# Counting out-degrees with node numbers split into 64 low and 100 high values, with three table copies on ScalarE

## The chip, the cores and the metric

The kernel runs on one core of one Trainium2 chip. The metric is the device time of one launch in microseconds (us). The time before is the median of three runs.

## The reference, cut to what matters

Four graph layers run one after the other on a graph of 6,250 nodes and 100,000 edges sorted by destination. The change touches only what the first layer needs of the sources: how many edges leave each node (`out_deg`), and the node features scaled with it.

```python
h = jnp.maximum(_layernorm(x, axis=-1), 0.0)
...
out_deg = jax.ops.segment_sum(ones_e, src, num_segments=N)
norm_src = jnp.clip(out_deg, 1.0, None) ** (-0.5)
h = nfeat * norm_src[:, None]
agg = jax.ops.segment_sum(h[src], dst, num_segments=N)
```

## The kernel before, in words

The program is a row of stages with a barrier between them: `survey` (statistics of the graph), `sort_edges` (skipped for sorted input), `tables` (the stage of the change), `gather_first` (the first layer over edge tiles), then three more layers. A stage is written out engine by engine; each engine works through its own list in order, and semaphores hold it where it needs another's result. A wait therefore also holds everything that stands behind it in the same list.

`tables` does three things at once.

**The out-degree counter.** The 100,000 source numbers lie as 125 partitions by 800 columns. A number is split in a low part (7 bits, 128 values) and a high part (50 values). The columns go in 50 groups (`GR`) of 16 (`W`). For each group VectorE makes two tables of zeros and ones in bf16: `low` (125 x 128 x 16, L457) and `high` (125 x 50 x 16, L459). TensorE then multiplies, for each of the 16 columns, `low[:, :, k]` (stationary, 128 columns wide) with `high[:, :, k]` (moving, 50 columns; L429) and adds everything up in one PSUM tile: row = low part, column = high part, value = out-degree. Both tables have two buffers. The semaphore `built` tells TensorE that a group is ready, `counted` tells VectorE that a group's buffer is free again, so VectorE may be two groups ahead and no more.

**The edge tables.** GpSimd gathers source, destination and type of each edge tile into `raw` by 24 indirect DMAs (L383). When the counter has reached group 30 (`LAY`), VectorE makes the local destinations, a validity mask and the keys out of them (L467 to L478) and copies source and type to floating point (L480, L482). In the groups behind that, 31 to 38, TensorE also transposes one of eight blocks of these tables per group (three transposes, L439) into one of two PSUM buffers `pt`. ScalarE takes them out (L411 to L413, or L407 and L408 for one block) and says so with `taken`; from the third block on TensorE waits for `taken` before it transposes into a buffer that was used:

```python
if b >= 2:
    pe.wait_ge(taken, b - 1)
```

SyncE writes keys and local destinations to DRAM and reads the keys back (L360 to L367); they are read in the next stage.

**The normalised features.** ScalarE squares the features (L395); at group 24 (`EVEN`) VectorE finishes the variance (L463), ScalarE takes the root (L398), at group 26 VectorE makes scale and shift (L485, L486; semaphore `scaled`), and ScalarE writes the normalised features `g.h` in 50 instructions (L401). After the last group VectorE reads the degrees (L488), ScalarE takes the root, VectorE inverts it, and both write the scaled features, which SyncE sends to DRAM in ten transfers (L374). Then the next stage starts.

In ScalarE's list of this stage the order is: squares, root, the 50 normalising instructions, the copies out of the transposed blocks, root of the degrees, scaled features.

Of the kernel before, what the change touches and what calls it, by code (L numbers as in the profile page):

```python
# [5 lines left out]
P = 128  # L6
# [3 lines left out]
NW = 50  # L10
NP = NW * P
# [4 lines left out]
TB = 7  # L16
TA = TB * P
EP, EC = 125, E // 125
# [11 lines left out]
BF16 = mybir.dt.bfloat16  # L30
I32 = mybir.dt.int32
ALU = mybir.AluOpType
# [272 lines left out]
def tables(nc, g, sem, a, early, scratch):  # L305
# [3 lines left out]
    W = 16  # L309
    GR = EC // W  # L310
    B8 = TB + 1
    K = NW // 5
    EVEN, LAY = 24, 30
    with Stage(nc, "od") as od:
        si, part = g.sources, od.sb("part", [EP, EC], I32)
        lo, hi = od.sb("lo", [EP, EC], BF16), od.sb("hi", [EP, EC], BF16)
        lows, highs = od.sb("lows", [EP, P, W], BF16), od.sb("highs", [EP, NW, W], BF16)
        low, high = od.sb("low", [EP, 2, P, W], BF16), od.sb("high", [EP, 2, NW, W], BF16)
    g.acc0 = early.sb("acc0", [P, NW * (2 * D + RELS)])
    with Stage(nc, "tb") as st:  # L320
        raw = st.sb("raw", [P, B8, 3, P], I32)
        rawf = st.sb("rawf", [P, B8, 3, P])
        ok = st.sb("ok", [P, B8, P])
        keys = st.sb("keys", [P, TB, P])
        pads = st.sb("pads", [1, P])
        local = st.sb("local", [P, TB, P], BF16)
# [6 lines left out]
        (dv, built, counted, squared, evened, rooted, scaled, normed, asked, answered, scaled2, sent_a, sent_d,  # L333
         laid, turned, taken, keyed, kept, out) = (
            sem("tb_" + k) for k in ("dv", "built", "counted", "squared", "evened", "rooted", "scaled", "normed",
                                     "asked", "answered", "scaled2", "sent_a", "sent_d", "laid", "turned", "taken",
                                     "keyed", "kept", "out"))
        got = [sem(f"tb_got{k}") for k in range(3)]
# [6 lines left out]
        with nc.Block() as block:  # L345
            @block.sync
            def _(sp):
# [8 lines left out]
                sp.wait_ge(out, 64)  # L356
                sp.wait_ge(keyed, 1)
                for b in range(TB):
# [21 lines left out]
            def _(pool):  # L380
                for k in (1, 0, 2):
                    for b in range(B8):
                        pool.indirect_dma_start(raw[:, b, k, :], None, g.edges_d.rearrange("k (e one) -> (k e) one", one=1),  # L383
                                                bass.IndirectOffsetOnAxis(g.starti[:, b:b + 1], 0),
                                                element_offset=k * (E + P)).then_inc(got[k], 16)
                pool.wait_ge(counted, GR)
                nc.gpsimd.memset(g.acc0[:, :], 0.0)

            @block.scalar
            def _(act):  # L390
                act.wait_ge(evened, 1)
                for v in range(NW):
                    if v >= 4:
                        act.wait_ge(squared, v - 3)
                    nc.scalar.activation(junk[:, v % 4, :], g.x[:, v * D:(v + 1) * D], ACT.Square, bias=less[:, v:v + 1],  # L395
                                         accum_out=var[:, v:v + 1]).then_inc(squared, 1)
                act.wait_ge(evened, 2)
                nc.scalar.activation(rstd[:, :], var[:, :], ACT.Sqrt).then_inc(rooted, 1)  # L398
                act.wait_ge(scaled, 1)
                for v in range(NW):  # L400
# [23 lines left out]
            @block.tensor  # L424
            def _(pe):
                for i in range(GR):
                    pe.wait_ge(built, 2 * (i + 1))
                    for k in range(W):
                        mm = nc.tensor.matmul(ps[:, 0:NW], low[:, i % 2, :, k], high[:, i % 2, :, k],  # L429
                                              start=(i == 0 and k == 0), stop=(i == GR - 1 and k == W - 1))  # L430
                    mm.then_inc(counted, 1)
                    if LAY < i <= LAY + B8:
                        b = i - LAY - 1
                        if b == 0:
                            pe.wait_ge(laid, 1)
                        if b >= 2:
                            pe.wait_ge(taken, b - 1)
                        for k in range(3):
                            t = nc.tensor.transpose(pt[b % 2][:, k * P:(k + 1) * P], rawf[:, b, k, :], g.ident[:, :])  # L439
                        t.then_inc(turned, 1)  # L440

            @block.vector
            def _(dve):
                c = Chain(dve, dv)
                nc.vector.memset(pads[:, :], -5.0)
                nc.vector.tensor_scalar(less[:, :], g.total[:, :], -1.0 / D, None, ALU.mult).then_inc(evened, 1)
                nc.vector.tensor_copy(lows[:, :, :], g.iota[0:EP, :].unsqueeze(2).broadcast_to([EP, P, W]))
                c.step(nc.vector.tensor_copy(highs[:, :, :], g.iota[0:EP, 0:NW].unsqueeze(2).broadcast_to([EP, NW, W])))
                c.step(nc.vector.tensor_scalar(part[:, :], si[:, :], 127, None, ALU.bitwise_and))
                c.step(nc.vector.tensor_copy(lo[:, :], part[:, :]))  # L450
                c.step(nc.vector.tensor_scalar(part[:, :], si[:, :], 7, None, ALU.arith_shift_right))
                c.step(nc.vector.tensor_copy(hi[:, :], part[:, :]))
                for i in range(GR):
                    if i >= 2:
                        dve.wait_ge(counted, i - 1)
                    cols = slice(i * W, (i + 1) * W)
                    nc.vector.tensor_tensor(low[:, i % 2, :, :], lo[:, cols].unsqueeze(1).broadcast_to([EP, P, W]),  # L457
                                            lows[:, :, :], ALU.is_equal).then_inc(built, 1)
                    nc.vector.tensor_tensor(high[:, i % 2, :, :], hi[:, cols].unsqueeze(1).broadcast_to([EP, NW, W]),  # L459
                                            highs[:, :, :], ALU.is_equal).then_inc(built, 1)  # L460
# [3 lines left out]
                    if i == LAY:  # L464
                        dve.wait_ge(got[1], 16 * B8)
                        dl, keep = rawf[:, :, 1, :], ok[:, :, :]
# [8 lines left out]
                        c.step(nc.vector.tensor_tensor(keys[:, :, :], keys[:, :, :], ok[:, 0:TB, :], ALU.mult))  # L475
                        c.step(nc.vector.tensor_scalar(dl, dl, -1.0, None, ALU.add))
                        c.step(nc.vector.tensor_scalar(keys[:, :, :], keys[:, :, :], -1.0, None, ALU.add))
                        nc.vector.tensor_copy(local[:, :, :], rawf[:, 0:TB, 1, :]).then_inc(keyed, 1)  # L478
                        dve.wait_ge(got[0], 16 * B8)
                        c.step(nc.vector.tensor_copy(rawf[:, :, 0, :], raw[:, :, 0, :]))  # L480
                        dve.wait_ge(got[2], 16 * B8)
                        nc.vector.tensor_copy(rawf[:, :, 2, :], raw[:, :, 2, :]).then_inc(laid, 1)  # L482
                    if i == EVEN + 2:
# [3 lines left out]
                dve.wait_ge(counted, GR)  # L487
                nc.vector.tensor_scalar(nsrc[:, :], ps[:, 0:NW], 1.0, None, ALU.max).then_inc(asked, 1)  # L488
                dve.wait_ge(answered, 1)
# [2531 lines left out]
```

## Time and profile before

| | |
|---|---|
| median of three runs | 5985.34 us (5979.43 to 5990.69) |
| profiled execution, its own time | 5982.85 us |
| its span, first to last instruction | 5980.8 us |
| stage `tables` in the span | about 53.4 to 185.6 us |
| mean granted TensorE clock of the span | 0.756 |

PE is TensorE's matmul, PEld its weight load, DVE is VectorE, ACT ScalarE, POOL GpSimd, SP SyncE; a "q" behind an engine's name means its queue of commands. A timeline row gives start, length, engine, line, operation, the tiles as out<-in, the shape, and how many equal neighbours were merged (x32); in brackets stands the idle time of the engine ahead of it and who ended that. The length of merged rows runs from the first start to the last end. For PE the names are out<-moving,stationary.

### The profile page before, as it was taken

The numbers are of one execution on the slowest core, as the hardware profiler recorded it, in microseconds if no ns is written. First come the engines' busy times: TensorE is split into PE (matmuls) and PEld (weight loads), VectorE is DVE, ScalarE is ACT, GpSimd is POOL, SyncE is SP. The second block draws the span as 40 slices with busy tenths as digits, with TensorE's granted clock in tenths as the row PEclk, the third lists the DMA queues.
The fourth block names the chain that finished last, engine by engine and source line by source line (L and its number), as shares of the span: only waits on it lengthen the run. The fifth ranks groups of instructions, "written<-read, shape, count | busy, mean of one in ns | idle before, by whom it ended". The sixth has DMA issues, their size and how long they took to land. (4 is left out here: it accounts for less than half of the span.)

```text
span 5980.8 us, 86128 instructions
## 1 busy us (share of the span) xinstructions
PE 4163.3 (70%) x19030; PEld 3347.1 (56%) x19030; DVE 3779.2 (63%) x11775; ACT 1878.5 (31%) x4142; POOL 4008.9 (67%) x4191
## 2 busy tenths in 40 slices
PE   4788888857676775897878887444444447777776
PEld 4677777646666664444555555333333336666665
DVE  8555555557777777646666666344444447777775
ACT  5132222233334342463333332011111124444442
POOL 2677777757777774007777777577777767777773
PEclk9987778867777776997888888555555567777776
DMA  2544444434444445165555555222222254454453
GB/s 59 135 137 119 120 118 119 117 110 141 136 139 136 137 140 128 53 288 166 155 158 158 157 159 143 60 64 68 64 68 64 68 109 144 144 150 146 144 152 64
DMA packets 426775, 738.45 MB, mean 123 GB/s; under 512 B 100522, under 2 KB 280579, under 8 KB 419700
## 3 DMA queue, kind: packets, MB, share of 16 engines
q0 software_dynamic: 173200, 436.47, 27.8%
q1 hardware_dynamic: 244484, 289.62, 14.7%
q10 hardware_dynamic: 8592, 6.82, 0.4%
q8 instruction: 176, 2.88, 0.2%
q14 instruction: 323, 2.65, 0.1%
HBM read 613.55 MB, written 120.20 MB: 123 GB/s over the span
## 5 line engine op out<-in xcount | busy, mean ns | idle before, releaser
L1628 POOL DMA_INDIRECT xh<-pair_d,src_i x1658 | 1582.9, 955 | 571.1 <-issue 490.4
L2659 POOL DMA_INDIRECT l2e_rows<-msg_d,msg_i x829 | 788.1, 951 | 568.2 <-POOLq L61 315.9
L854 POOL DMA_INDIRECT l2f_rows<-msg_d,msg_i x829 | 785.4, 947 | 290.1 <-issue 239.2
L999 POOL DMA_INDIRECT l0e_rows<-node_d,src_i x829 | 789.8, 953 | 260.3 <-issue 222.9
L1156 PE MATMUL l0e_ps<-l0e_rows,l0e_sel 128*128 128x256 f32 x1664 | 712.0, 520 | 193.8 <-DVE early_acc L1223 76.4
L888 PE MATMUL l2f_ps<-l2f_rows,l2f_sel 128*128 128x128 f32 x1664 | 427.3, 423 | 579.6 <-DVE l2f_sel L907 359.9
L888 PEld LDWEIGHTS l2f_ps<-l2f_rows,l2f_sel 128*128 128x128 f32 x1664 | 372.5, 315 | 661.9 <-DVE l2f_sel L907 399.5
L2793 PE MATMUL l2e_ps<-l2e_rows,l2e_sel 128*128 128x256 f32 x1664 | 550.6, 461 | 80.6 <-DVE l2e_sel L2885 38.2
L1223 DVE TENSOR_TENSOR early_acc<-early_acc,l0e_ps 128x264 f32 x832 | 356.3, 428 | 335.8 <-PE l0e_ps L1157 262.1
L919 DVE TENSOR_TENSOR xh<-xh,l2f_ps 128x128 f32 x832 | 238.8, 287 | 519.3 <-PE l2f_ps L888 413.1
L2850 DVE TENSOR_TENSOR l_acc<-l_acc,l2e_ps 128x256 f32 x832 | 349.1, 420 | 325.5 <-PE l2e_ps L2793 321.8
L1672 PE MATMUL l1te_pq<-l1t_queries,l1te_wide 128*128 x1664 | 328.5, 360 | 287.6 <-DVE l1te_prod L1903 276.7
L1672 PE MATMUL l3te_pq<-l3t_queries,l3te_wide 128*128 x1664 | 326.8, 359 | 258.1 <-DVE l3te_prod L1903 236.8
L1672 PEld LDWEIGHTS l1te_pq<-l1t_queries,l1te_wide 128*128 128x128 f32 x1664 | 283.1, 257 | 334.2 <-issue 334.0
L2793 PEld LDWEIGHTS l2e_ps<-l2e_rows,l2e_sel 128*128 128x128 f32 x1664 | 342.3, 226 | 227.7 <-issue 69.6
L1156 PEld LDWEIGHTS l0e_ps<-l0e_rows,l0e_sel 128*128 128x128 f32 x1664 | 329.5, 243 | 229.8 <-issue 180.6
L1157 PEld LDWEIGHTS l0e_ps<-l0e_of_rel,l0e_sel 128*128 128x128 f32 x1664 | 409.5, 246 | 84.0
L1672 PEld LDWEIGHTS l3te_pq<-l3t_queries,l3te_wide 128*128 128x128 f32 x1664 | 282.6, 257 | 298.1 <-issue 296.7
L1724 PE MATMUL l1te_ps<-l1te_ve,l1te_sel 128*128 128x144 f32 x1664 | 365.6, 377 | 11.0 <-DVE l1te_ve L2016 10.7
L2032 DVE TENSOR_TENSOR l1acc_acc<-l1acc_acc,l1te_ps 128x144 f32 x832 | 246.5, 296 | 168.5 <-PE l1te_ps L1724 161.6
L2032 DVE TENSOR_TENSOR l_acc<-l_acc,l3te_ps 128x130 f32 x832 | 234.3, 282 | 171.4 <-PE l3te_ps L1724 167.9
L1724 PEld LDWEIGHTS l1te_ps<-l1te_ve,l1te_sel 128*128 128x128 f32 x1664 | 320.3, 266 | 19.7 <-DVE l1te_ve L2016 13.5
(463 smaller groups left out, 8336.5 us busy)
## 6 DMA issues: line engine op xcount, KB each, us to landing
l0e_rows<-in_edge_attr_dram SPq DMA_DIRECT2D x832, 64.0 KB
msg_d<-l1t_queries SPq DMA_DIRECT2D x50, 1024.0 KB, 3.9
l1te_local<-local_d SPq DMA_DIRECT2D x52, 512.0 KB
l2e_local<-local_d SPq DMA_DIRECT2D x52, 512.0 KB
l3te_local<-local_d SPq DMA_DIRECT2D x52, 512.0 KB
xh<-pair_d,src_i POOLq DMA_INDIRECT x1658, 2.8
msg_d<-l2e_msg SPq DMA_DIRECT2D x50, 512.0 KB
l0e_rows<-node_d,src_i POOLq DMA_INDIRECT x829
```

Of the source, the lines that this page charges most:

```text
L854: pool.indirect_dma_start(rows[:, t % R, :], None, table, bass.IndirectOffsetOnAxis(index[:, t:t + 1], 0)) \
L888: nc.tensor.matmul(ps[t % B][:, 0:D], sel[:, n % V, t % G, :], rows[:, t % R, :], start=True, stop=True).then_inc(summed, 1)
L999: pool.indirect_dma_start(rows[:, t % R, 0:D], None, table, bass.IndirectOffsetOnAxis(g.src_i[:, t:t + 1], 0)).then_inc(gathered[t % R], 16)
L1156: nc.tensor.matmul(ps[r % B][:, 0:2 * D], sel[:, r // G % 2, r % G, :], rows[:, r, :], start=True, stop=True)
L1157: nc.tensor.matmul(ps[r % B][:, 2 * D:W0], sel[:, r // G % 2, r % G, :], of_rel[:, r // G % 2, r % G, :], start=True, stop=True).then_inc( ...
L1223: nc.vector.tensor_tensor(one, one, ps[s][:, 0:W0], ALU.add).then_inc(added, 1)
L1628: pool.indirect_dma_start(rows[:, t % R, :], None, g.pair_d, bass.IndirectOffsetOnAxis(g.src_i[:, t:t + 1], 0)).then_inc(gathered[n % RG], 16)
L1672: mm = nc.tensor.matmul(pq[n % 2][:, i * D:(i + 1) * D], wide[:, n // GS % 2, n % GS * G + i, :], queries[:, bass.ds(ws[i] * D, D)], start ...
L1724: nc.tensor.matmul(slot(t), sel[:, n % V, t % G, :], ve[:, n % V, t % G, :], start=True, stop=True).then_inc(summed, 1)
L2032: nc.vector.tensor_tensor(part, part, slot(t), ALU.add).then_inc(added, 1)
L2659: pool.indirect_dma_start(rows[:, t % R, :], None, table, bass.IndirectOffsetOnAxis(index[:, t:t + 1], 0)).then_inc(gathered[t % R], 16)
L2793: nc.tensor.matmul(ps[t % B][:, 0:width], sel[:, t // G % 2, t % G, :], rows[:, t % R, :], start=True, stop=True).then_inc(summed, 1)
```

## The change

The numbers are split into 64 low values (6 bits) and 100 high values. `low` becomes 125 x 64 x 16 and `high` 125 x 100 x 16; a matmul has a stationary operand of 64 columns and a moving one of 100, and its result is 64 x 100. After the last group VectorE copies that result to SBUF (`tally`), and TensorE spreads it to the 128 x 50 layout that the rest uses by two float32 matmuls: even columns with the identity, odd columns with `beyond`, an identity shifted by 64 rows. VectorE reads the degrees from there.

Three copies of the edge tables move from VectorE's block at group 30 to ScalarE: source and type to floating point, placed ahead of the root, and the local destinations to bf16, placed between the root and the 50 normalising instructions. Semaphore `laid` goes; `based`, `widened`, `tallied` and `merged` come; `keyed` now counts to two.

```diff
+    LOW = 64
+    HIGH = NP // LOW
...
-                sp.wait_ge(keyed, 1)
+                sp.wait_ge(keyed, 2)
...
+                for k in (0, 2):
+                    act.wait_ge(got[k], 16 * B8)
+                    nc.scalar.copy(rawf[:, :, k, :], raw[:, :, k, :]).then_inc(widened, 1)
                 act.wait_ge(evened, 2)
                 nc.scalar.activation(rstd[:, :], var[:, :], ACT.Sqrt).then_inc(rooted, 1)
+                act.wait_ge(based, 1)
+                nc.scalar.copy(local[:, :, :], rawf[:, 0:TB, 1, :]).then_inc(keyed, 1)
                 act.wait_ge(scaled, 1)
                 for v in range(NW):
                     nc.scalar.activation(g.h[:, v * D:(v + 1) * D], g.x[:, v * D:(v + 1) * D], ACT.Relu,
...
-                        mm = nc.tensor.matmul(ps[:, 0:NW], low[:, i % 2, :, k], high[:, i % 2, :, k],
+                        mm = nc.tensor.matmul(ps[0:LOW, 0:HIGH], low[:, i % 2, :, k], high[:, i % 2, :, k],
                                               start=(i == 0 and k == 0), stop=(i == GR - 1 and k == W - 1))
...
                         if b == 0:
-                            pe.wait_ge(laid, 1)
+                            pe.wait_ge(based, 1)
+                            pe.wait_ge(widened, 2)
...
+                pe.wait_ge(tallied, 1)
+                nc.tensor.matmul(ps[:, P:P + NW], g.ident[0:LOW, :], tally[:, 0::2], start=True, stop=False)
+                nc.tensor.matmul(ps[:, P:P + NW], beyond[:, :], tally[:, 1::2], start=False, stop=True).then_inc(merged, 1)
...
+                nc.vector.tensor_scalar(beyond[:, :], g.iota[0:LOW, :], g.tile_f[0:LOW, 0:1], float(LOW), ALU.subtract,
+                                        ALU.is_equal)
-                nc.vector.tensor_copy(lows[:, :, :], g.iota[0:EP, :].unsqueeze(2).broadcast_to([EP, P, W]))
+                nc.vector.tensor_copy(lows[:, :, :], g.iota[0:EP, 0:LOW].unsqueeze(2).broadcast_to([EP, LOW, W]))
...
-                    nc.vector.tensor_tensor(low[:, i % 2, :, :], lo[:, cols].unsqueeze(1).broadcast_to([EP, P, W]),
+                    nc.vector.tensor_tensor(low[:, i % 2, :, :], lo[:, cols].unsqueeze(1).broadcast_to([EP, LOW, W]),
                                             lows[:, :, :], ALU.is_equal).then_inc(built, 1)
-                    nc.vector.tensor_tensor(high[:, i % 2, :, :], hi[:, cols].unsqueeze(1).broadcast_to([EP, NW, W]),
+                    nc.vector.tensor_tensor(high[:, i % 2, :, :], hi[:, cols].unsqueeze(1).broadcast_to([EP, HIGH, W]),
                                             highs[:, :, :], ALU.is_equal).then_inc(built, 1)
...
-                        c.step(nc.vector.tensor_scalar(dl, dl, -1.0, None, ALU.add))
-                        c.step(nc.vector.tensor_scalar(keys[:, :, :], keys[:, :, :], -1.0, None, ALU.add))
-                        nc.vector.tensor_copy(local[:, :, :], rawf[:, 0:TB, 1, :]).then_inc(keyed, 1)
-                        dve.wait_ge(got[0], 16 * B8)
-                        c.step(nc.vector.tensor_copy(rawf[:, :, 0, :], raw[:, :, 0, :]))
-                        dve.wait_ge(got[2], 16 * B8)
-                        nc.vector.tensor_copy(rawf[:, :, 2, :], raw[:, :, 2, :]).then_inc(laid, 1)
+                        nc.vector.tensor_scalar(dl, dl, -1.0, None, ALU.add).then_inc(based, 1)
+                        nc.vector.tensor_scalar(keys[:, :, :], keys[:, :, :], -1.0, None, ALU.add).then_inc(keyed, 1)
...
                 dve.wait_ge(counted, GR)
-                nc.vector.tensor_scalar(nsrc[:, :], ps[:, 0:NW], 1.0, None, ALU.max).then_inc(asked, 1)
+                nc.vector.tensor_copy(tally[:, :], ps[0:LOW, 0:HIGH]).then_inc(tallied, 1)
+                dve.wait_ge(merged, 1)
+                nc.vector.tensor_scalar(nsrc[:, :], ps[:, P:P + NW], 1.0, None, ALU.max).then_inc(asked, 1)
```

## Rows read from the trace of the kernel before

**Rows 1.** Windows view: busy us of each engine, granted clock, DMA share, GB/s.

```profile
119.00:130.00 11.00, 0.29 (x3) 0.21 (x3) 10.69 (x14) 10.87 (x29) 0.00 (x0) 1.00 0.09 25
```

**Rows 2.** Groups by line, 40 to 230 us: busy us, mean ns | idle before.

```profile
L429 PE MATMUL tb_ps<-od_high,od_low 125*128 125x50 bf16 x800 | 86.0, 281 | 36.9 <-DVE od_high L459 36.5
...
L457 DVE TENSOR_TENSOR od_low<-od_lo,od_lows 125x2048 bf16<-125x2048 bf16 x50 | 61.2, 1224 | 12.3 <-PE tb_ps L429 8.3 <-DMA edges_d<-sv_padi 4.0
...
L459 DVE TENSOR_TENSOR od_high<-od_hi,od_highs 125x800 bf16<-125x800 bf16 x50 | 28.4, 569 | 0.0
```

**Rows 3.** Timeline of DVE, one group of the counting loop.

```profile
79.42 1.23 DVE L457 TENSOR_TENSOR od_low<-od_lo,od_lows 125x2048 bf16<-125x2048 bf16 x1 [0.23 <-PE tb_ps L429]
```

**Rows 4.** Timeline of PE in the counting loop.

```profile
77.61 3.40 PE L429 MATMUL tb_ps<-od_high,od_low 125*128 125x50 bf16 x32 [0.17 <-DVE od_high L459]
81.19 3.41 PE L429 MATMUL tb_ps<-od_high,od_low 125*128 125x50 bf16 x32 [0.18 <-DVE od_high L459]
...
132.03 1.77 PE L429 MATMUL tb_ps<-od_high,od_low 125*128 125x50 bf16 x16
...
134.25 1.76 PE L429 MATMUL tb_ps<-od_high,od_low 125*128 125x50 bf16 x16
...
165.44 1.79 PE L429 MATMUL tb_ps<-od_high,od_low 125*128 125x50 bf16 x16 [0.20 <-DVE od_high L459]
```

**Rows 5.** Windows view of L1156, the next stage's matmul: PE, PEld, granted clock, DMA.

```profile
200.00:210.00 10.00, 8.68 (x16) 3.86 (x15) 1.00 0.55 148
...
370.00:380.00 10.00, 5.50 (x18) 2.45 (x17) 1.00 0.51 148
...
390.00:400.00 10.00, 9.37 (x16) 4.16 (x15) 0.50 0.51 140
```

**Rows 6.** Timeline of PE in a later stage: float32 matmuls of 256 and 512 columns.

```profile
3011.18 1.46 PE L2793 MATMUL l2e_ps<-l2e_rows,l2e_sel 128*128 128x256 f32 x6
3012.48 1.88 PE L2778 MATMUL l2e_pm<-l2e_w,l2e_ht 128*128 128x512 f32 x4
3014.20 1.03 PE L2793 MATMUL l2e_ps<-l2e_rows,l2e_sel 128*128 128x256 f32 x4
```

**Rows 7.** L2746, bf16 weights of 128 columns, 8 moving: timeline.

```profile
2962.53 0.41 PE L2746 MATMUL l2e_pn<-l2e_counts,l2e_selt 128*128 x8
```

**Rows 8.** L2746 by its own view: ns min/median/max.

```profile
L2746 PE MATMUL l2e_pn<-l2e_counts,l2e_selt x832: 172/181/228, 2706.7 to 3727.5; 128*128 x167
```

**Rows 9.** Timeline of DVE: the block at group 30.

```profile
117.19 1.08 DVE L467 TENSOR_SCALAR tb_keys<-tb_raw 128x896 f32<-128x896 int32 x1
...
124.32 0.69 DVE L476 TENSOR_SCALAR tb_rawf<-tb_rawf 128x1024 f32<-128x1024 f32 x1
...
125.71 1.08 DVE L478 CAST tb_local<-tb_rawf 128x896 bf16<-128x896 f32 x1
...
128.04 1.22 DVE L457 TENSOR_TENSOR od_low<-od_lo,od_lows 125x2048 bf16<-125x2048 bf16 x1
```

**Rows 10.** Timeline of ACT in the same stage.

```profile
106.35 0.25 ACT L398 ACTIVATE tb_rstd<-tb_var 128x50 f32<-128x50 f32 x1 [31.88 <-DVE tb_var L463]
110.48 19.39 ACT L401 ACTIVATE xh<-xh,tb_shift,tb_rstd 128x128 f32<-128x128 f32 x50 [3.88 <-DVE tb_shift L486]
132.28 0.27 ACT L411 CAST src_i<-tb_pt 128x128 int32<-128x128 f32 x1 [2.41 <-PE tb_pt L439]
...
132.60 0.29 ACT L413 COPY rel<-tb_pt 128x128 f32<-128x128 f32 x1
```

**Rows 11.** Timeline of ACT in a later stage, long rows.

```profile
2699.66 11.24 ACT L2695 ACTIVATE l_acc<-iota 128x2560 f32<-128x2560 f32 x5 [7.33 <-PEq L61]
```

**Rows 12.** Timeline of the survey: a small float32 matmul and its reader.

```profile
40.05 0.74 PE L199 MATMUL sv_ps<-sv_wide,ones 50*128 50x100 f32 x2 [3.94 <-DVE sv_wide L261]
...
40.83 0.21 DVE L263 COPY sv_begin<-sv_ps 128x50 f32<-128x50 f32 x1 [0.84 <-PE sv_ps L199]
```

**Rows 13.** Timeline of SP: the keys read back.

```profile
135.27 3.72 SPq L367 DMA_DIRECT2D early_key<-keys_d  x7
```

More of the change, by code:

```diff
@@ L316, in tables @@
         lo, hi = od.sb("lo", [EP, EC], BF16), od.sb("hi", [EP, EC], BF16)
-        lows, highs = od.sb("lows", [EP, P, W], BF16), od.sb("highs", [EP, NW, W], BF16)
-        low, high = od.sb("low", [EP, 2, P, W], BF16), od.sb("high", [EP, 2, NW, W], BF16)
+        lows, highs = od.sb("lows", [EP, LOW, W], BF16), od.sb("highs", [EP, HIGH, W], BF16)
+        low, high = od.sb("low", [EP, 2, LOW, W], BF16), od.sb("high", [EP, 2, HIGH, W], BF16)
     g.acc0 = early.sb("acc0", [P, NW * (2 * D + RELS)])
@@ L325, in tables @@
         pads = st.sb("pads", [1, P])
+        beyond, tally = st.sb("beyond", [LOW, P]), st.sb("tally", [LOW, HIGH])
         local = st.sb("local", [P, TB, P], BF16)
@@ L333, in tables @@
         (dv, built, counted, squared, evened, rooted, scaled, normed, asked, answered, scaled2, sent_a, sent_d,
-         laid, turned, taken, keyed, kept, out) = (
+         turned, taken, keyed, kept, out, based, widened, tallied, merged) = (
             sem("tb_" + k) for k in ("dv", "built", "counted", "squared", "evened", "rooted", "scaled", "normed",
-                                     "asked", "answered", "scaled2", "sent_a", "sent_d", "laid", "turned", "taken",
-                                     "keyed", "kept", "out"))
+                                     "asked", "answered", "scaled2", "sent_a", "sent_d", "turned", "taken",
+                                     "keyed", "kept", "out", "based", "widened", "tallied", "merged"))
         got = [sem(f"tb_got{k}") for k in range(3)]
@@ L446, in _ @@
                 nc.vector.tensor_scalar(less[:, :], g.total[:, :], -1.0 / D, None, ALU.mult).then_inc(evened, 1)
-                nc.vector.tensor_copy(lows[:, :, :], g.iota[0:EP, :].unsqueeze(2).broadcast_to([EP, P, W]))
-                c.step(nc.vector.tensor_copy(highs[:, :, :], g.iota[0:EP, 0:NW].unsqueeze(2).broadcast_to([EP, NW, W])))
-                c.step(nc.vector.tensor_scalar(part[:, :], si[:, :], 127, None, ALU.bitwise_and))
+                nc.vector.tensor_scalar(beyond[:, :], g.iota[0:LOW, :], g.tile_f[0:LOW, 0:1], float(LOW), ALU.subtract,
+                                        ALU.is_equal)
+                nc.vector.tensor_copy(lows[:, :, :], g.iota[0:EP, 0:LOW].unsqueeze(2).broadcast_to([EP, LOW, W]))
+                c.step(nc.vector.tensor_copy(highs[:, :, :], g.iota[0:EP, 0:HIGH].unsqueeze(2).broadcast_to([EP, HIGH, W])))
+                c.step(nc.vector.tensor_scalar(part[:, :], si[:, :], LOW - 1, None, ALU.bitwise_and))
                 c.step(nc.vector.tensor_copy(lo[:, :], part[:, :]))
-                c.step(nc.vector.tensor_scalar(part[:, :], si[:, :], 7, None, ALU.arith_shift_right))
+                c.step(nc.vector.tensor_scalar(part[:, :], si[:, :], 6, None, ALU.arith_shift_right))
                 c.step(nc.vector.tensor_copy(hi[:, :], part[:, :]))
```

## The prediction

> **What bounds the kernel now.** I read the windows first. The stage takes some 132 us of 5981, so the change can only matter by microseconds. While VectorE makes the edge tables, TensorE stands almost still: 0.29 of 11 us busy, VectorE 10.69, ScalarE 10.87 [rows 1]. The groups by line come next: VectorE's two comparisons take 1.22 and 0.57 us per group, fifty times, and it waits for TensorE 8.3 us in all, TensorE for it 36.5 [rows 2]. Neither engine is simply full, so I went to the timelines for the loop's clockwork. A low table starts at 79.42 [rows 3], its group's matmuls at 81.19, 1.77 us later; from a group's first matmul (77.61) to the low table that takes its buffer again (79.42) pass 1.81 us [rows 3, 4]. The sum, 3.58, is the distance between PE's bursts (77.61 to 81.19), in which two groups pass. The loop is thus bound by one buffer's round trip, build plus consume, at 1.79 us a group, with VectorE idle only 0.23 us a pair [rows 3]. Where transposes run in between, a group takes 132.03 to 134.25, 2.22 us, and TensorE is the bound [rows 4].
>
> One matmul of the loop: 32 take 3.40 us, the last lasts 0.281 [rows 2, 4], so (3.40 - 0.28) / 31 = 0.100 us each, 16 take 1.60, and three transposes 2.22 - 1.60 = 0.62.
>
> **TensorE's clock.** The clock column says 1.00 for 200 to 210 us, yet 16 matmuls of L1156 take 8.68 us there. That is like 390 to 400, granted 0.50 (16 in 9.37), and unlike 370 to 380, granted 1.00 (18 in 5.50) [rows 5]. I take the early part of the span as running at the lower level, 1.2 GHz, whatever the column says, and the loop with it: 0.100 us are then 120 cycles.
>
> **The change, part by part.**
>
> *Building.* From 2048 and 800 elements in 1.224 and 0.569 us [rows 2], an element costs 0.655 / 1248 = 0.525 ns. A low table of 1024 takes 0.69 us, a high one of 1600 takes 0.99: 1.68 instead of 1.79, 0.12 saved per group. The set-up before the loop (half of one table, double the other, one small `beyond`) comes out even, and a 4.0 us stall behind it that VectorE does not owe to TensorE [rows 2] would swallow the difference; I leave it at its place, so groups 0 to 3 gain nothing.
>
> *One matmul.* No row shows 64 bf16 weight columns and 100 moving ones. L2746 loads 128 bf16 columns and streams 8: eight in 0.41 us, the last 0.18 [rows 7, 8], 0.033 each, which at 2.4 GHz are 79 cycles. The loop's 120 cycles have 42 more moving columns and 41 more cycles: here load and stream add up, 71 for the load, one for each column. The float32 rows are of another kind: six matmuls of 256 columns take 3011.18 to 3012.48, 0.217 us each, four of 512 take 3012.48 to 3014.20, 0.43 each [rows 6]; twice the columns, twice the time, and each has its own load, so there the load hides behind the stream. The ends are a hidden load, 100 columns at 1.2 GHz, 0.083 us, and an added one of unchanged length, (71 + 100) / 1.2 = 0.142 us. I take 0.085: the new stream of 100 columns is longer than the load of 71 cycles, as in those rows; in the loop until now it was shorter, 50 against 71. The Trainium skill (TensorE: Matmul & The Clock Gate, "Weight-path perf modes") says that the fast weight load is on only with 128 weight columns of a type other than float32; halving the columns would then lose it. At the page's rate for ordinary loads, one column per 1.2 GHz cycle, 64 columns are an estimated 53 ns, hardly less than the 59 ns (71 cycles) found here for 128; added to the stream that makes 0.137 us a matmul and some 29 us more for the kernel, hidden it makes my figure. No run here shows either yet.
>
> *The loop.* 16 matmuls take 1.36 instead of 1.60. Round trip: 1.77 - 0.12 + 1.81 - 0.24 = 3.22, 1.61 us a group, 0.18 saved. (VectorE's own floor, 3.58 - 0.23 - 0.24 = 3.11 a pair, is close below.) Groups 4 to 29 save 26 x 0.18 = 4.7 us, group 30's build 0.1: VectorE's block starts at 117.19 - 4.8 = 112.4 [rows 9].
>
> *The block.* Three casts leave, 125.71 to 128.04, 2.3 us [rows 9]. `based` comes after L476, 124.32 + 0.69 - 117.19 = 7.8 us into the block, at 120.2; group 31's tables start 8.5 into it, at 120.9.
>
> *The three copies.* ScalarE takes 11.24 / 5 = 2.25 us for 2560 columns [rows 11], 0.88 ns each: 0.9 to 1.0 us per copy. Those of source and type lie in the 31.88 us in which it idles ahead of the root [rows 10] and cost nothing: the root is asked for at 106.35 - 20 x 0.18 = 102.7. Should the gathers land so late that this cover is gone, they cost up to 2 us ahead of group 26. The copy of the local destinations is different. It waits for `based` at group 30, and behind it in ScalarE's list stand the 50 normalising instructions, 19.39 us, which until now ran from 110.48 and so were over when the first block had been transposed [rows 10], and then the copies out of PSUM, 0.61 us a block (132.28 to 132.60 + 0.29) [rows 10]. The first `taken` comes at 120.2 + 0.1 + 0.9 + 19.4 + 0.6 = 141.2. TensorE waits for it ahead of the third block: it starts group 31 at 120.9 + 1.65 = 122.6 and has three groups and two triples behind it at 122.6 + 4.8 + 1.2 = 128.6. So it stands for 12.6 us, and VectorE, two groups ahead, with it. This is the change's main cost, and it eats what the loop saves.
>
> *After it.* One triple, 0.62, then five groups with transposes at 1.36 + 0.62 = 1.98, then eleven at 1.61: 28.2 us, the counter ends at 169.4. Before it ended at 165.44 + 1.79 = 167.23 [rows 4]: 2.2 us later.
>
> *The merge.* Copying 100 columns from PSUM, 0.25 by L263's 0.21 for 50, then two float32 matmuls: the first with its reader 40.05 to 40.83, 0.78 [rows 12], the second half of 0.74 and some, 0.43; a hand-over 0.06: 1.5 us, all on the path. The merge could cost as little as half of that, or 2.5 with longer hand-overs.
>
> *Queues.* SyncE waits for `keyed` at two, about 121, earlier than now; its reading back is issued by 139 now [rows 13], and its next work, the ten feature transfers, follows the degrees. Nobody waits there. GpSimd's clearing of `acc0` starts with the last count as now.
>
> **The sum.** +2.2 + 1.5 = +3.7 us on the profiled execution's 5982.85 (span 5980.8 and 2 us around it), 5986.6. That execution lies 2.5 below the median of the runs, 5985.34, so I say 5989. Its own range, for matmuls of 0.083 to 0.095 us and hand-overs, is 5983 to 5995. About 0.2%, 12 us, is what a measurement of this kernel can tell from no change.
>
> **The rivals.**
>
> *The matmuls become slower (the other side).* Place: L429. If the load is added to the stream, a matmul takes 0.142 us and a group 2.28, bound by TensorE. The block then starts 26 x 0.49 later, less 0.1, at 129.8, `taken` comes at 158.6, and 0.62 + 5 x 2.90 + 11 x 2.28 = 40.2 more gives 198.8: +31.6 + 1.5 = +33, 6018. For: load and stream add up in both bf16 rows here. Against: the float32 rows. The page's rule named above, a fast load that 64 columns lose, would end here if the ordinary load is not hidden. It decides from 0.107 us a matmul on, where the sum reaches 12 us (0.38 us for each ns).
>
> *The matmul changes little.* At the old 0.100 (an issue rate, not columns) a group takes 1.73: block at 115.5, `taken` at 144.3, counter at 175.1, +9.4 with the merge, 5995. With a load that halves but still adds, (36 + 100) / 1.2 = 0.113: +14.5, 6000.
>
> *The clock rises in the loop.* A busier stream may bring 2.4 GHz; rows 5 show such a rise between 210 and 370 us, not its cause. A matmul near 0.045 leaves VectorE the bound at 1.56: block 111.1, `taken` 139.9, 25.6 more, 165.5, merge 1.2: about -0.5, 5985. Even this ideal gains nothing that can be told, as the 19.39 us stand behind `based`.
>
> *ScalarE's list does not hold TensorE.* Then 122.6 + 8 x 1.98 + 11 x 1.61 = 156.1, -9.6 in all, 5976. The order of the list and the wait for `taken` speak against it.
>
> **How the numbers follow.** Forecast 0.58; slower matmuls at 0.142, 0.13; little change 0.15, half of that on each of its figures; clock 0.10; no hold 0.04. From 5979 to 6004 the range holds all but the first and the last rival, 0.17, with the bounds of the merge; the matmul's upper end is the first rival itself. Slower by over 0.2%: 0.13, the 0.113 figure's 0.07, and 0.02 of the forecast's tail, 0.22. Faster: 0.03, mostly of the last rival. Within: 0.75.
>
> **What would show it.** Bursts of 32 matmuls of 2.9 us in the loop (0.085 each); VectorE's tables 0.69 and 0.99; the 50 normalising instructions starting behind the copy of `local`, near 121; a PE gap of some 12 us at L439's third block, ended by ScalarE's L413; the last count near 169 and the first degree operation 1.5 later. I am wrong if the burst takes over 3.4 us, if the gap is missing, or if a later stage moves by more than the shift.

## The result, and the profile after

The changed kernel takes 6054.78 us (median of four runs, 6044.93 to 6059.03), the kernel before 5988.01 beside it (5979.43 to 5992.28): 1.0104 times as long, with a 95% interval of 1.0091 to 1.0116. The forecast was 5989 with a range from 5979 to 6004, so the prediction was wrong. The profiled execution has a span of 6043.0 us, 62.2 more than before. All of that arises in the stage of the change: its first operation on the degrees starts at 230.06 us (the line stands below), against 167.26 before, and the following stages together differ by 0.6 us. The line of before, from VectorE's timeline:

```profile
167.26 0.21 DVE L488 TENSOR_SCALAR tb_nsrc<-tb_ps 128x50 f32<-128x50 f32 x1 [1.88 <-PE tb_ps L429]
```

First the windows of the kernel after, in the columns of [rows 1]; the first row is the loop up to group 30, the second the stretch of the transposes, the third the last eleven groups.

```profile
59.70:146.80 87.10, 87.08 (x474) 87.08 (x475) 48.28 (x64) 17.02 (x74) 23.44 (x21) 1.00 0.12 19
...
156.70:196.00 39.30, 31.75 (x152) 26.85 (x153) 13.34 (x18) 22.04 (x68) 0.00 (x0) 1.00 0.10 27
196.00:228.60 32.60, 32.59 (x177) 32.25 (x176) 15.21 (x19) 0.60 (x3) 0.00 (x0) 1.00 0.00 1
```

TensorE is busy without a break, 87.08 of 87.10 us, and VectorE little more than half the time. The round trip that bound the loop before is gone: TensorE alone is the bound. The groups by line, 40 to 290 us, say the same from the other side and answer to [rows 2].

```profile
L437 PE MATMUL tb_ps<-od_high,od_low 125*64 125x100 bf16 x800 | 149.6, 364 | 24.6 <-DVE od_high L473 24.6
...
L473 DVE TENSOR_TENSOR od_high<-od_hi,od_highs 125x1600 bf16<-125x1600 bf16 x50 | 49.2, 984 | 0.0
L471 DVE TENSOR_TENSOR od_low<-od_lo,od_lows 125x1024 bf16<-125x1024 bf16 x50 | 34.6, 691 | 77.9 <-PE tb_ps L437 77.9
```

VectorE's tables cost 0.691 and 0.984 us, as worked out, but it now waits 77.9 us for TensorE instead of 8.3. The timeline of TensorE gives the pace, that is the time from one matmul to the next, and answers to [rows 4].

```profile
59.72 91.41 PE L437 MATMUL tb_ps<-od_high,od_low 125*64 125x100 bf16 x496 [19.05 <-DVE od_high L473]
156.72 3.19 PE L437 MATMUL tb_ps<-od_high,od_low 125*64 125x100 bf16 x16 [5.59 <-DVE od_high L473]
...
164.63 3.19 PE L437 MATMUL tb_ps<-od_high,od_low 125*64 125x100 bf16 x16
175.36 0.90 PE L448 MATMUL tb_pt<-ident,tb_rawf 128*128 128x128 f32 x3 [7.53 <-ACT rel L421]
176.20 3.20 PE L437 MATMUL tb_ps<-od_high,od_low 125*64 125x100 bf16 x16
...
180.16 3.19 PE L437 MATMUL tb_ps<-od_high,od_low 125*64 125x100 bf16 x16
...
196.00 32.59 PE L437 MATMUL tb_ps<-od_high,od_low 125*64 125x100 bf16 x176
228.94 0.66 PE L451 MATMUL tb_ps<-tb_tally,ident 64*128 64x50 f32 x2 [0.35 <-DVE tb_tally L497]
```

The 176 matmuls of the last eleven groups take 32.59 us, the last one 0.364: (32.59 - 0.364) / 175 = 0.184 us each. Before it was 0.100. A group takes 16 x 0.184 = 2.94 us, and 3.96 with a triple of transposes (176.20 to 180.16).

The timelines of VectorE and of ScalarE hold the other steps; the VectorE rows answer to [rows 9], the ScalarE rows to [rows 10].

```profile
146.79 1.08 DVE L481 TENSOR_SCALAR tb_keys<-tb_raw 128x896 f32<-128x896 int32 x1
...
155.07 0.68 DVE L471 TENSOR_TENSOR od_low<-od_lo,od_lows 125x1024 bf16<-125x1024 bf16 x1
...
228.63 0.25 DVE L497 COPY tb_tally<-tb_ps 64x100 f32<-64x100 f32 x1 [4.29 <-PE tb_ps L437]
230.06 0.21 DVE L499 TENSOR_SCALAR tb_nsrc<-tb_ps 128x50 f32<-128x50 f32 x1 [1.18 <-PE tb_ps L452]
```

```profile
154.66 0.94 ACT L406 CAST tb_local<-tb_rawf 128x896 bf16<-128x896 f32 x1 [25.04 <-DVE tb_rawf L490]
155.50 19.34 ACT L409 ACTIVATE xh<-xh,tb_shift,tb_rstd 128x128 f32<-128x128 f32 x50
...
175.05 0.26 ACT L421 COPY rel<-tb_pt 128x128 f32<-128x128 f32 x1
```

**Where the 62.8 us come from.** VectorE's block starts 29.6 us later than in [rows 9] (146.79 against 117.19): 26 groups at 2.94 instead of 1.79 are 29.9. The block itself is 2.6 shorter (146.79 to 155.07, 8.28, against 10.85). From there to the last count pass 73.5 us instead of 39.2. Of these 34.3, 7.5 are the gap in which TensorE waits for ScalarE; eight groups with transposes at 3.96 instead of 2.22 are 13.9, eleven without at 2.94 instead of 1.79 are 12.7. The merge adds 1.5. The slower matmul alone makes 1.15 us in 37 of these 45 groups and 1.34 (2.94 instead of 1.60) in the eight with transposes, 53 of the 62.8 us: the stage hangs on one number.

### The profile page after: what moved, and what is told of

It is laid out like the page before. It is cut to its first block and busy times, and to the rows that moved or that the text cites. A ratio compares the mean times of both kernels' runs of the same rounds, so it can differ in the third digit from the quotient of the medians.

```text
span 6043.0 us, 86138 instructions
## 1 busy us (share of the span) xinstructions
PE 4216.0 (70%) x19034; PEld 3399.9 (56%) x19034; DVE 3773.7 (62%) x11774; ACT 1880.5 (31%) x4145; POOL 4002.5 (66%) x4191
## 5 line engine op out<-in xcount | busy, mean ns | idle before, releaser
L1167 PE MATMUL l0e_ps<-l0e_rows,l0e_sel 128*128 128x256 f32 x1664 | 686.0, 504 | 215.8 <-DVE early_acc L1234 95.7
L1168 PEld LDWEIGHTS l0e_ps<-l0e_of_rel,l0e_sel 128*128 128x128 f32 x1664 | 394.5, 237 | 78.1
L1735 PE MATMUL l1te_ps<-l1te_ve,l1te_sel 128*128 128x144 f32 x1664 | 362.2, 374 | 12.4 <-DVE l1te_ve L2027 12.1
L1735 PE MATMUL l3te_ps<-l3te_ve,l3te_sel 128*128 128x130 f32 x1664 | 321.6, 348 | 14.0 <-DVE l3te_ve L2027 7.8
```

Source lines behind the costliest of these rows:

```text
L1167: nc.tensor.matmul(ps[r % B][:, 0:2 * D], sel[:, r // G % 2, r % G, :], rows[:, r, :], start=True, stop=True)
L1168: nc.tensor.matmul(ps[r % B][:, 2 * D:W0], sel[:, r // G % 2, r % G, :], of_rel[:, r // G % 2, r % G, :], start=True, stop=True).then_inc( ...
L1735: nc.tensor.matmul(slot(t), sel[:, n % V, t % G, :], ve[:, n % V, t % G, :], start=True, stop=True).then_inc(summed, 1)
```

## The experiments

Paces are worked out as above, from the length of merged rows. The theories that the expectations name: LOAD (64 weight columns lose a fast load, and the longer load is added to the stream), STREAM (the streamed columns set the pace, at some two cycles each), then STRIDE (a column costs about twice as much, streamed or loaded, because its neighbour lies 32 bytes away: the tables are `[EP, value, W]`, so neighbouring values of one k are 16 bf16 elements apart) and FAST LOAD (only a load of exactly 128 bf16 columns escapes that price). Times of single runs stand beside a run of the kernel before on the same chip: 5983.95 us for the first four kernels, 5983.54 for the next four, 5982.32 (median of 18) for the last three.

### The change taken apart

**Half the stream.** The changed kernel, but only 50 of the 100 moving columns are streamed.

```diff
-mm = nc.tensor.matmul(ps[0:LOW, 0:HIGH], low[:, i % 2, :, k], high[:, i % 2, :, k],
+mm = nc.tensor.matmul(ps[0:LOW, 0:NW], low[:, i % 2, :, k], high[:, i % 2, 0:NW, k],
...
```

> The changed kernel with only 50 of the 100 moving columns streamed (same tables built; the high values 50 to 99 are left out of the count). Measured so far: 120 cycles of 1.2 GHz per matmul with 128 weight and 50 moving columns, 220 with 64 and 100. Theory LOAD (the load of 64 columns takes some 120 cycles where that of 128 took 70, and load and stream add up): 120 + 50 = 170 cycles, 0.142 us a matmul, a group every 2.27 us. Theory STREAM (the load is hidden, a moving column takes two cycles and a matmul 20 besides): back to 120 cycles, 0.100 us a matmul, a group every 1.73 us.

Measured: 6003.6 us. TensorE's timeline, the last eleven groups:

```profile
163.33 21.35 PE L437 MATMUL tb_ps<-od_high,od_low 125*64 125x50 bf16 x176
```

That is (21.35 - 0.301) / 175 = 0.120 us, neither of the two forecasts. More than half of the excess is gone with half the stream, so the stream matters; but 50 columns with 64 weights are slower than 50 with 128 (0.100), so something of the load shows as well.

**The wide stream with the old weights.** The kernel before with `high` twice as wide (the upper half never matches), so 128 weight columns and 100 moving ones.

```diff
-mm = nc.tensor.matmul(ps[:, 0:NW], low[:, i % 2, :, k], high[:, i % 2, :, k],
+mm = nc.tensor.matmul(ps[:, 0:2 * NW], low[:, i % 2, :, k], high[:, i % 2, :, k],
...
-high = od.sb("high", [EP, 2, NW, W], BF16)
+high = od.sb("high", [EP, 2, 2 * NW, W], BF16)
...
```

> The kernel before with the high table and the stream 100 columns wide, the upper 50 all zeros, so the result is the same. LOAD: 70 + 100 = 170 cycles, 0.142 us a matmul, a group every 2.27 us. STREAM: 20 + 200 = 220 cycles, 0.184 us, a group every 2.94 us, as in the changed kernel.

Measured: 6045.42 us. TensorE's timeline, the last eleven groups:

```profile
191.98 33.36 PE L429 MATMUL tb_ps<-od_high,od_low 125*128 125x100 bf16 x176
```

(33.36 - 0.37) / 175 = 0.189 us. The slowdown is there with the weights as they were. LOAD's 0.142 missed, STREAM's 0.184 came; the pace of the changed kernel is that of its stream.

**The split alone.** The split and the merge, with the three copies back in VectorE's block.

```diff
-                nc.scalar.copy(local[:, :, :], rawf[:, 0:TB, 1, :]).then_inc(keyed, 1)
...
+                        nc.vector.tensor_copy(local[:, :, :], rawf[:, 0:TB, 1, :]).then_inc(keyed, 1)
...
```

> The changed split and its merge, the three copies back on VectorE. Both theories of the matmul: 0.184 us, 2.94 us a group. The gap of 7.5 us at the third transposed block goes, VectorE's block is 2.3 us longer: the last count at about 224 us (changed kernel 228.6), the span about 6038. If instead the copies on ScalarE were the cause of the loss, the last count would be back near 170.

Measured: 6041.62 us, 57.7 over its neighbour. The pace is the same:

```profile
191.21 32.59 PE L432 MATMUL tb_ps<-od_high,od_low 125*64 125x100 bf16 x176
```

The last count comes at 223.8, where 224 was expected. The split carries the loss; the copies are worth some microseconds either way.

**The copies alone.** The old split of 128 and 50, the three copies on ScalarE as in the change.

```diff
+                act.wait_ge(based, 1)
+                nc.scalar.copy(local[:, :, :], rawf[:, 0:TB, 1, :]).then_inc(keyed, 1)
                 act.wait_ge(scaled, 1)
...
```

> The old split, the three copies on ScalarE as in the change. If ScalarE's list holds TensorE: a gap of about 12 us at the third transposed block, ended by ScalarE's copy of rel, the last count at about 177 us (before 167.2), the span about 5991. If it does not: no gap, the last count near 165, the span about 5978.

Measured: 6000.09 us, one run. TensorE's timeline, the third transposed block and the last group:

```profile
145.21 0.90 PE L445 MATMUL tb_pt<-ident,tb_rawf 128*128 128x128 f32 x3 [12.33 <-ACT rel L418]
...
174.93 1.77 PE L434 MATMUL tb_ps<-od_high,od_low 125*128 125x50 bf16 x16 [0.18 <-DVE od_high L465]
```

The hold is 12.33 us, where the prediction had 12.6, and the last count comes at 176.7, 9.5 after that of [rows 4]. The span is 17 longer; the other 7.6 us lie in later stages, and one run can't say whether they belong to this kernel.

### Is it the spacing?

**The moving operand side by side.** The changed kernel; the 100 moving columns are taken as neighbours from the same buffer. The weights stay 32 bytes apart.

```diff
-mm = nc.tensor.matmul(ps[0:LOW, 0:HIGH], low[:, i % 2, :, k], high[:, i % 2, :, k],
+mm = nc.tensor.matmul(ps[0:LOW, 0:HIGH], low[:, i % 2, :, k],
+                      high[:, i % 2, :, :].rearrange("p v k -> p (v k)")[:, k * HIGH:(k + 1) * HIGH],
```

> The changed kernel, each matmul's 100 moving columns taken side by side (a slice of the same table) and no longer 32 bytes apart; the weights stay 32 bytes apart. The slices do not belong together, so the counts are not degrees; instructions and sizes are the same. Known: 0.184 us with 100 moving columns, 0.120 with 50 (64 weight columns). Theory STRIDE (a column 32 bytes from the next costs some 2.2 cycles, beside it one; load and stream overlap, the longer one sets the pace): the stream falls to about 100 cycles, the load of 64 columns is then the longer with about 144 cycles, 0.120 us, a group every 1.92 us. Theory COLUMN (2.2 cycles whatever the layout): 0.184 us, 2.94 us a group.

Measured: 6007.94 us. TensorE's timeline, the last eleven groups:

```profile
163.88 21.43 PE L437 MATMUL tb_ps<-od_high,od_low 125*64 125x100 bf16 x176
```

(21.43 - 0.32) / 175 = 0.121 us, as STRIDE forecast. With as many columns and as many bytes as in the changed kernel a third of a matmul's time is gone. It stands where half the stream stood (0.120): what is the same in both is the load of 64 columns 32 bytes apart, and the next run takes that away.

**Both operands side by side.** The weights are taken in the same way, beside the edit above.

```diff
-low[:, i % 2, :, k],
+low[:, i % 2, :, :].rearrange("p v k -> p (v k)")[:, k * LOW:(k + 1) * LOW],
```

> As e5, and the 64 weight columns side by side as well (counts again not degrees). STRIDE: load about 64 to 70 cycles, stream 100, so 0.083 to 0.09 us a matmul, 16 in 1.4 us, and the loop bound by the round trip at about 1.6 us a group. COLUMN: 0.184 us, 2.94 us a group.

Measured: 5981.42 us. TensorE's timeline, the start of the loop, two later groups and the third transposed block:

```profile
60.25 3.05 PE L437 MATMUL tb_ps<-od_high,od_low 125*64 125x100 bf16 x32 [19.34 <-DVE od_high L474]
...
84.13 0.91 PE L437 MATMUL tb_ps<-od_high,od_low 125*64 125x100 bf16 x16 [0.60 <-DVE od_high L474]
...
120.19 1.54 PE L437 MATMUL tb_ps<-od_high,od_low 125*64 125x100 bf16 x16 [8.87 <-DVE od_high L474]
...
138.82 0.91 PE L449 MATMUL tb_pt<-ident,tb_rawf 128*128 128x128 f32 x3 [12.61 <-ACT rel L421]
```

The first 32 go at (3.05 - 0.295) / 31 = 0.089 us, with the hand-over between their two groups in it; a group by itself (120.19) goes at (1.54 - 0.295) / 15 = 0.083, one cycle of 1.2 GHz for each of 100 columns and close to the prediction's 0.085. In between a matmul takes about half of that, (0.91 - 0.204) / 15 = 0.047: TensorE has gone from the lower clock level to the higher one and back. The granted clock reads 0.50 from 120 to 125 us, and 1.00 from 144 to 149 us, where groups again take 0.91 us. At the higher level VectorE is the bound. The hold stands with 12.61 us.

**The kernel before with its moving operand side by side.** The first of these edits, on L429.

```diff
-high[:, i % 2, :, k],
+high[:, i % 2, :, :].rearrange("p v k -> p (v k)")[:, k * NW:(k + 1) * NW],
```

> The kernel before with the 50 moving columns side by side (counts not degrees), weights of 128 columns 32 bytes apart as before, 0.0995 us a matmul. If the stream of 50 sets the pace there (2.2 x 50 = 110 cycles and some): the matmul falls to what the load of 128 takes, below 0.0995; STRIDE with a fast load guesses 0.06 to 0.08. If the load does: 0.0995 again.

Measured: 5970.90 us. TensorE's timeline, one group:

```profile
84.72 1.20 PE L429 MATMUL tb_ps<-od_high,od_low 125*128 125x50 bf16 x16 [0.43 <-DVE od_high L460]
```

(1.20 - 0.238) / 15 = 0.064 us instead of 0.100. So the kernel before was held by its strided stream of 50 columns too, and its load of 128 strided columns takes 0.064 us or less.

**One weight column less.** The kernel before with 127 of the 128 weight columns; low value 127 is left out, and VectorE fills the result tile once ahead of the loop.

```diff
-mm = nc.tensor.matmul(ps[:, 0:NW], low[:, i % 2, :, k], high[:, i % 2, :, k],
+mm = nc.tensor.matmul(ps[0:P - 1, 0:NW], low[:, i % 2, 0:P - 1, k], high[:, i % 2, :, k],
...
```

> The kernel before with 127 of the 128 weight columns (nodes whose low value is 127 are left out of the count). Theory FAST LOAD (only a full 128 is loaded the quick way; otherwise 144 / 64 = 2.25 cycles a column as with 64): 127 x 2.25 = 286 cycles, 0.238 us a matmul, 3.8 us a group, the span some 85 us longer. Theory COLUMNS (the load goes by columns alone): 0.0995 us as before, the span as before.

Measured: 6067.17 us. TensorE's timeline, the first 31 groups:

```profile
60.07 117.82 PE L429 MATMUL tb_ps<-od_high,od_low 125*127 125x50 bf16 x496 [19.24 <-DVE od_high L460]
```

(117.82 - 0.42) / 495 = 0.237 us against 0.100 with 128: FAST LOAD hit. Without it 127 columns cost 1.87 ns each; the 64 of the changed kernel cost 0.120 us, 1.88 ns each, and 100 streamed ones 0.184 us, 1.84 each.

### What can be had

**The copies alone, the local one late.** As "the copies alone", but the copy of the local destinations stands behind the copies out of the third transposed block.

```diff
-                act.wait_ge(based, 1)
-                nc.scalar.copy(local[:, :, :], rawf[:, 0:TB, 1, :]).then_inc(keyed, 1)
...
+                    if b == 2:
+                        nc.scalar.copy(local[:, :, :], rawf[:, 0:TB, 1, :]).then_inc(keyed, 1)
...
```

> The old split, the three copies on ScalarE, but the copy of the local destinations behind ScalarE's copies out of the third transposed block instead of ahead of the 50 normalising instructions. If the place in ScalarE's list made the 12.3 us gap: these instructions start at group 26 again and the gap shrinks to under 1 us; VectorE's block is 2.3 us shorter than before, the last count at about 165 us (before 167.2, copies ahead 176.7). If the copies themselves cost it (a slower ScalarE, a later table): the gap stays.

Measured: 5986.44 us, one run. TensorE's timeline, the third transposed block and the last group:

```profile
133.17 0.83 PE L445 MATMUL tb_pt<-ident,tb_rawf 128*128 128x128 f32 x3
...
162.79 1.79 PE L434 MATMUL tb_ps<-od_high,od_low 125*128 125x50 bf16 x16 [0.19 <-DVE od_high L465]
```

No hold, and the last count at 164.6: 12.1 us earlier than with the early copy and 2.6 earlier than before. The place in ScalarE's list was the whole cost of the hold. The time of this one run doesn't show the 2.6 us.

**The same, with the high table in pairs.** Neighbouring values of one k lie 4 bytes apart; the columns of the group are taken two by two.

```diff
-high = od.sb("high", [EP, 2, NW, W], BF16)
+high = od.sb("high", [EP, 2, W // 2, NW, 2], BF16)
...
-mm = nc.tensor.matmul(ps[:, 0:NW], low[:, i % 2, :, k], high[:, i % 2, :, k],
+mm = nc.tensor.matmul(ps[:, 0:NW], low[:, i % 2, :, k], high[:, i % 2, k // 2, :, k % 2],
...
+nc.vector.tensor_tensor(high[:, i % 2, :, :, :],
+    hi[:, cols].rearrange("p (a b) -> p a b", b=2).unsqueeze(2).broadcast_to([EP, W // 2, NW, 2]),
+    highs[:, :, :].unsqueeze(1).broadcast_to([EP, W // 2, NW, 2]), ALU.is_equal)
...
```

> As e9, and the high table laid out in pairs of columns, so that the 50 moving columns are 4 bytes apart and no longer 32; the result is the same as before. STRIDE (spacing of the columns costs): a matmul near 0.064 us as in e7, VectorE the bound at 1.62 us a group, the last count near 154 us, the run some 13 us (0.2%) shorter than before. If 4 bytes cost as much as 32: 0.0995 us a matmul and some 2 us shorter. If VectorE loses its pace on pairs (569 to some 990 ns a high table): 2.05 us a group and the run some 10 us longer.

Measured: 5971.15 us (median of 11), 0.9979 of the kernel before [0.9970, 0.9988]. The timelines of TensorE and of VectorE, a group and a transposed block before 128 us, the same behind it, the last group, and a high table:

```profile
125.77 1.18 PE L434 MATMUL tb_ps<-od_high,od_low 125*128 125x50 bf16 x16
126.77 0.88 PE L445 MATMUL tb_pt<-ident,tb_rawf 128*128 128x128 f32 x3
...
128.46 0.52 PE L445 MATMUL tb_pt<-ident,tb_rawf 128*128 128x128 f32 x3
...
133.74 1.18 PE L434 MATMUL tb_ps<-od_high,od_low 125*128 125x50 bf16 x16
134.76 0.53 PE L445 MATMUL tb_pt<-ident,tb_rawf 128*128 128x128 f32 x3
...
151.57 1.20 PE L434 MATMUL tb_ps<-od_high,od_low 125*128 125x50 bf16 x16 [0.42 <-DVE od_high L465]
```

```profile
80.36 0.57 DVE L465 TENSOR_TENSOR od_high<-od_hi,od_highs 125x800 bf16<-125x800 bf16 x1
```

A pace of 0.064 us again: 4 bytes apart is as good as side by side, and VectorE writes the table in this order at its old 0.57 us.

**The change with both tables in pairs and the late copy.** The two edits above, on the changed kernel.

```diff
-low, high = od.sb("low", [EP, 2, LOW, W], BF16), od.sb("high", [EP, 2, HIGH, W], BF16)
+low, high = od.sb("low", [EP, 2, W // 2, LOW, 2], BF16), od.sb("high", [EP, 2, W // 2, HIGH, 2], BF16)
...
-low[:, i % 2, :, k], high[:, i % 2, :, k],
+low[:, i % 2, k // 2, :, k % 2], high[:, i % 2, k // 2, :, k % 2],
...
```

> The changed kernel with both tables in pairs (columns 4 bytes apart) and the copy of the local destinations placed as in e9; the result is the same as before. STRIDE: a matmul of 0.083 to 0.09 us at 1.2 GHz, as in e6, VectorE the bound at 1.50 us a group, no gap over 2 us at the third block, the first degree operation near 154 us, the run some 13 us shorter than before. If 4 bytes cost as much as 32: 0.184 us a matmul, as long as the changed kernel less the 7.5 us gap. If VectorE loses its pace on pairs: about 3 us a group.

Measured: 5966.67 us (median of 8), 0.9973 of the kernel before [0.9963, 0.9984], 88 us less than the changed kernel. The timelines of TensorE and of VectorE:

```profile
58.97 3.05 PE L437 MATMUL tb_ps<-od_high,od_low 125*64 125x100 bf16 x32 [18.24 <-DVE od_high L474]
...
75.67 0.91 PE L437 MATMUL tb_ps<-od_high,od_low 125*64 125x100 bf16 x16 [0.59 <-DVE od_high L474]
...
117.75 1.54 PE L437 MATMUL tb_ps<-od_high,od_low 125*64 125x100 bf16 x16 [8.87 <-DVE od_high L474]
...
146.54 0.91 PE L437 MATMUL tb_ps<-od_high,od_low 125*64 125x100 bf16 x16 [0.59 <-DVE od_high L474]
147.79 0.42 PE L451 MATMUL tb_ps<-tb_tally,ident 64*128 64x50 f32 x2 [0.35 <-DVE tb_tally L499]
```

```profile
80.04 0.69 DVE L471 TENSOR_TENSOR od_low<-od_lo,od_lows 125x1024 bf16<-125x1024 bf16 x1
80.64 0.99 DVE L474 TENSOR_TENSOR od_high<-od_hi,od_highs 125x1600 bf16<-125x1600 bf16 x1
81.54 0.69 DVE L471 TENSOR_TENSOR od_low<-od_lo,od_lows 125x1024 bf16<-125x1024 bf16 x1
```

The same 64 and 100 columns now go at 0.089 us (0.083 in a group by itself, 117.75) and at 0.047 at the higher clock level, and VectorE, which waits for TensorE 1.3 us in all of the loop, sets the pace with 1.50 us a group (80.04 to 81.54). The last count is at 147.5 instead of 228.6, and the first operation on the degrees starts at 148.5, where 154 was expected. This is the lowest median of all versions: what the smaller tables save on VectorE arrives once TensorE keeps up and the copy is out of the way.

## Why the prediction was wrong

**The step that failed is "One matmul".** The sum went by 0.085 us, one cycle of 1.2 GHz for each of 100 moving columns with the load hidden; 0.184 was measured. The price of one cycle comes from the sentence "here load and stream add up, 71 for the load, one for each column". They don't add up. The pace is the longer of load and stream: with 64 strided weight columns it is 0.120 us with either of two streams that are shorter (50 strided columns, 0.100 in the kernel before; 100 close ones, 0.083). And at the lower clock level a streamed column cost 1.84 ns with its neighbour 32 bytes away, 0.83 with it 4 bytes away or next to it. The kernel before was bound by its strided stream of 50 columns (0.100 us; 0.064 once they lie side by side), not by a load of 71 cycles plus 50. The change doubled that stream, and 0.100 became 0.184. Both ends of the stated bound, 0.083 and 0.142, assumed one cycle per moving column, so the truth lay outside of the range. The plainest reading of [rows 4], that the 50 columns alone set the 0.100 us, gives 0.20 us for 100 and was not among the rivals.

That sentence rests on L2746 [rows 7, 8], and its row was misread. It does not stream 8 columns (x8 counts merged rows): the code takes `K3` of them, with `K3 = 3 * RELS` and `RELS = 8`, so 24. Nor does it run at 2.4 GHz there: the granted clock reads 0.50 from 2962.50 to 2962.95 us, and six matmuls of L2793 take 2.46 us just before, against 1.46 a little later, where the granted clock reads 1.00 (2964.9 to 2966.2).

```profile
2960.27 2.46 PE L2793 MATMUL l2e_ps<-l2e_rows,l2e_sel 128*128 128x256 f32 x6
...
2964.81 1.46 PE L2793 MATMUL l2e_ps<-l2e_rows,l2e_sel 128*128 128x256 f32 x6
```

The 0.033 us are then 39 cycles and not 79, for 24 columns and not 8. Against L429, 26 columns more would cost 81 cycles more, and the agreement of 42 columns with 41 cycles was luck. The two rows differ in layout as well: L2746 takes both operands side by side, L429 takes both 32 bytes apart.

The spacing was in the code: both operands are read with k as the last index of a tile that is `W` = 16 long.

**A second loss hides behind the first.** With 64 weight columns 32 bytes apart the load takes 0.120 us (half the stream; the moving operand side by side), at the price of a column that the 127 show, 1.88 and 1.87 ns; with 128 the load takes 0.064 us or less. Side by side the 64 are hidden behind the stream, so their load takes at most 0.083 us; how much less no run shows. In the changed kernel the stream of 0.184 covers it. The rival "the matmuls become slower" thus had the right side and the right engine, but the wrong mechanism and price: with the load added it gave 0.142 and 6018.

The Trainium skill (TensorE: Matmul & The Clock Gate, "Weight-path perf modes") ties the fast load to exactly 128 weight columns of a type other than float32, and says that it reads four chunks of 32 columns at once. The trace agrees: 0.237 us with 127 columns, 0.100 with 128. An estimate from that page and the 1.88 ns of a strided column, 32 x 1.88 = 0.060 us, stands close to the 0.064 that the kernel before shows with its moving columns side by side.

The Trainium skill (SBUF — State Buffer, "Specifications (TRN2)") gives 16-byte lines of which an access pattern has to hit each at least twice to read at full bandwidth. The paces agree, 1.84 to 2.0 ns a streamed column at 32 bytes (100 and 50 of them), 0.83 at 4 bytes or side by side. The distances between 4 and 32 bytes were not tried, so the runs don't show where the limit lies. This rule was not weighed in the prediction, though it speaks against this change.

**The rest of the working held**, which is seen when its sum is done again with 0.184. The block comes at 117.2 + 26 x (2.94 - 1.79) - 0.1 = 147.0 (measured 146.79). The third block goes on 28.8 later, at 175.8 (measured 175.36). With 0.62 + 5 x 3.56 + 11 x 2.94 = 50.8 more the last count would be at 226.6 (measured 228.59; the 2 us are triples, which cost 1.02 and not 0.62 in a group of the new split, for a reason that stays open; spacing alone isn't it, as from a triple to the next group pass 0.83 us with the 64 columns side by side too, at the lower level, and 0.65 with 127 strided ones). The merge was forecast with 1.5 us and took 1.47 (228.59 to 230.06).

- *Building*: 0.69 and 0.99 forecast, 0.691 and 0.984 measured.
- *The three copies*: 0.94 us for the local one, the 50 normalising instructions right behind it at 155.50, and the gap at the third block, ended by ScalarE's copy out of PSUM. Its 12.6 us came as 12.33 and 12.61 where the loop was fast, and as 7.53 in the changed kernel, because the slower TensorE had more of its own work left before that point: three groups and two triples, 10.9 us instead of 6.0. That the order of ScalarE's list makes the gap is shown by the late copy, without a gap.
- *The clock* had not risen by the end of the changed kernel's loop: the merge's first matmuls, 0.35 us behind the last eleven groups, take 0.66 us there (228.94) and 0.42 in the last kernel above (147.79). Among its transposes it had not either: they take 0.90 us a triple, as in the last kernel from 118 to 123 us, where the granted clock reads 0.50; from 124 us on, where it reads 1.00, they take 0.55. No row shows the level of its first 31 groups, which go at 0.184 us as well. It did rise in the two kernels in which 64 and 100 columns lie close, and the rival's pace near 0.045 came as 0.047; with 128 weight columns and a close stream of 50 the transposes show a rise too.

Not settled: what makes the clock rise in these kernels and not in the changed one, and whether the later stages of the single runs with the copies alone (7.6 us too long) belong to them.

## What to carry to other kernels

Before a matmul is costed by its columns, look at how far apart the columns lie: a streamed bf16 column 32 bytes from its neighbour cost 1.84 to 2.0 ns here, one 4 bytes away 0.83 and less, and a layout in pairs gave TensorE this price while VectorE still wrote its tables at full speed. When two rows of different lines fit one formula, check that they have the same access pattern, and take the number of columns and the clock of each from its own row or code, before the formula is used for a third. A copy that moves to an idle engine also moves into that engine's order: ask what stands behind its wait.

## What the runs showed of the hardware beyond the question

A weight load of 127 bf16 columns instead of 128, 32 bytes apart, takes a matmul from 0.100 to 0.237 us.

The 0.064 us of the pair layout with 128 weight columns doesn't follow TensorE's clock: its triples of transposes fall from 0.88 to 0.53 us, while the 16 matmuls beside them take 1.18 us before and after (125.77 and 133.74). It isn't the stream that sets it: 50 columns at 0.83 ns are an estimated 0.042 us, and less at the higher level. What is left is the load of 128 columns 32 bytes apart (L2746, side by side, goes at 0.033 us), which would then be paced by something other than that clock; no run tries that load by itself. Whether the strided stream follows the clock was not seen: where the level of those kernels shows, it is the lower one.

The clock column reads 1.00 for the loop of the changed kernel (windows above), and for the pair layout both from 58.9 to 62 us, where 32 matmuls take 3.05 us, and from 74 to 82 us, where 16 take 0.91: that column alone doesn't tell the level there.
